# Sums of operands merged, the resolvent done by pairs, and the up product's second sum moved from ScalarE and GpSimd to VectorE

## What is computed

```python
def _s4_kernel(Lambda, p, q, B, Ct, step, L):
    g = 2.0 / step * ((1.0 - Omega) / (1.0 + Omega))
    denom = g[:, None] - Lambda[None, :]
    cauchy = lambda v: (v[None, :] / denom).sum(-1)
...
    at_roots = c * (k00 - k01 * (1.0 / (1.0 + k11)) * k10)
    return jnp.fft.ifft(at_roots, L).real
...
    g = jnp.einsum('bsh,ih->bsi', x, Wg)
    u = jnp.einsum('bsh,ih->bsi', x, Wu)
    h = jax.nn.silu(g) * u
    return jnp.einsum('bsi,hi->bsh', h, Wd)
```

## Time and profile before

| | |
|---|---|
| median of 3 runs | 1396.7 us (1395.41 to 1397.81) |
| the profiled execution | 1395.57 us, of which the span is 1393.4 us |
| TensorE busy | 1313.1 us, 94% |
| VectorE busy | 975.8 us, 70%; 98% from 200 to 500 us |
| ScalarE busy | 463.0 us, 33% |
| GpSimd busy | 687.9 us, 49%, all of it before 926 us |
| mean granted TensorE clock | 0.982 |

### The profile page before, as it was taken

One profiled execution on the slowest core, in us unless ns is written; L12 is line 12 of the kernel. 1 busy time (PEld: TensorE's weight loads), 2 busy tenths in 40 slices (PEclk: granted clock), 3 DMA queues, 4 the chain that ended last, 5 costly groups with the idle time before them and its releaser, 6 DMA issues.

```text
span 1393.4 us, 17064 instructions
## 1 busy us (share of the span) xinstructions
PE 1313.1 (94%) x6302; PEld 623.3 (45%) x6302; DVE 975.8 (70%) x1036; ACT 463.0 (33%) x827; POOL 687.9 (49%) x483
## 2 busy tenths in 40 slices
PE   3688899999999999899999999899999999999998
PEld 2444344444444444344444444344444444444444
DVE  7966799999999998879999898524343433241432
ACT  5744544455444455344454543410000000000000
POOL 6772777878787777668788896620000000000000
PEclk8799999999999999999999999999999999999999
DMA  8111545454555445444645543999554345336331
GB/s 311 34 46 38 165 142 155 133 179 140 168 146 162 138 136 175 117 155 130 179 137 176 157 144 114 334 414 310 165 189 149 98 151 183 104 109 219 99 98 61
DMA packets 165168, 218.09 MB, mean 157 GB/s; under 512 B 42204, under 2 KB 122718, under 8 KB 163166
## 3 DMA queue, kind: packets, MB, share of 16 engines
q1 hardware_dynamic: 163646, 200.69, 46.4%
q10 hardware_dynamic: 1440, 16.32, 2.9%
HBM read 139.64 MB, written 77.34 MB: 156 GB/s over the span
## 4 chain that ended last, share of the span: by engine, by line
PE 57%; DVE 3%; issue 1%; ACT 1%; DMA 0%; POOL 0%; SPq 0%; ACTq 0%; DVEq 0%
PE px L1461 16%; PE px L1375 13%; PE pz L1461 8%; PE pz L1375 6%; PE pv L1488 6%; PE py L1461 4%; PE py L1375 3%; DVE wf L1575 1%; DMA w_d<-ds 0%; DVE wf L1546 0%; DVE wf L1543 0%; DVE wf L1617 0%; DVE hf L1673 0%; DVE hf L1676 0%; POOL ds L696 0%
## 5 line engine op out<-in xcount | busy, mean ns | idle before, releaser
L1375 PE MATMUL px<-xo,wo 128*128 128x512 f16 x2016 | 464.2, 384 | 28.0 <-ACT u L997 21.3
L1375 PEld LDWEIGHTS px<-xo,wo 128*128 128x128 f16 x2016 | 197.4, 99 | 273.9 <-issue 26.0
L687 POOL TENSOR_TENSOR wo<-wf,wo 128x512 f16<-128x512 f32 x147 | 235.9, 1614 | 70.4 <-ACT wo L943 70.4
L706 POOL TENSOR_TENSOR hs<-hf,hs 128x512 f16<-128x512 f32 x154 | 215.4, 1405 | 108.5 <-ACT hs L978 108.3
L1461 PE MATMUL px<-wd,hr 128*128 128x512 f16 x1056 | 232.3, 379 | 0.0
L1375 PE MATMUL pz<-xo,wo 128*128 128x512 f16 x1008 | 231.3, 379 | 0.1
L1461 PEld LDWEIGHTS px<-wd,hr 128*128 128x128 f16 x1056 | 102.3, 98 | 118.7
L1375 PEld LDWEIGHTS pz<-xo,wo 128*128 128x128 f16 x1008 | 98.6, 98 | 118.4 <-issue 0.4
L943 ACT ACTIVATE wo<-wf 128x512 f16<-128x512 f32 x147 | 91.6, 624 | 102.5 <-DVE wf L1547 92.5
L978 ACT ACTIVATE hs<-hf 128x512 f16<-128x512 f32 x154 | 94.5, 621 | 89.6 <-DVE hf L1639 47.6
L1461 PE MATMUL pz<-wd,hr 128*128 128x512 f16 x528 | 116.6, 379 | 0.0
(11 more groups left out here) (229 smaller groups left out, 1417.4 us busy)
## 6 DMA issues: line engine op xcount, KB each, us to landing
h_d<-hs SPq DMA_DIRECT2D x154, 256.0 KB, 2.6
hr<-h_d SPq DMA_DIRECT2D x56, 704.0 KB, 4.4
w_d<-ds SPq DMA_DIRECT2D x73, 256.0 KB, 2.1
wd<-w_d ACTq DMA_DIRECT2D x4, 2816.0 KB, 15.5
sz<-in_sz_gate SPq DMA_DIRECT2D x21, 512.0 KB, 5.1
sz<-in_sz_up SPq DMA_DIRECT2D x21, 512.0 KB, 4.8
sz<-in_sz_down SPq DMA_DIRECT2D x20, 512.0 KB, 5.1
xc_d<-xo SPq DMA_DIRECT2D x8, 1024.0 KB, 7.6
```

The source lines that it names most:

```text
L687: pool.tensor_tensor(w_dest(t, j, 1), w_place_of(j), w_dest(t, j, 0), ALU.subtract).then_inc(wlo_done, 1)
L706: pool.tensor_tensor(hs[:, j, :, 1, :], h_place_of(p, j), hs[:, j, :, 0, :], ALU.subtract)\
L1375: done = pe.matmul(bank[:, :], wo[t % 2][:, j, wp, k * P:(k + 1) * P], xo[p][:, j, xp, k, :], start=(j in (0, 3) and k == 0 and wp == 0 an ...
```

## The change

1. **c22 to VectorE.** snap_u3 on ScalarE and the sum on GpSimd are gone. VectorE adds px (after turn 5) and s5 into u3 itself. TensorE's turn 7, which writes over px, now waits for this instruction. It stands behind s4_work(n) and ahead of c12(n).
2. **Fewer sums.** T1 and T3 of the weights are made by one instruction of twice the width, for gate and up and for down; so are S1 and S2 of h (h_s12, which now also waits for what only its second half waited for). S3 is taken with the other sign.
3. **Resolvent by pairs.** Two pieces at once, at n = 6, 11, 16 and 21, in seven instructions of 128x256. What follows comes a unit later: roots at 25, columns at 27, rows at 29, scale at 32. The angles are loaded in pairs.
4. **Tail.** The mask of the last words (`tail_words`) is a tensor_tensor with a tile of fifteens in place of a tensor_scalar.

```diff
             def c22(n):
-                pool.wait_ge(snap_done, 4 * full(n) + 4)
-                pool.tensor_tensor(u3[:, :], u3[:, :], s5[:, :], ALU.add).then_inc(u2_done, 1)
...
-            def snap_u3(n):
-                act.wait_ge(prod_done, products_before(n) + TURN_POS[4] + 1)
-                if n >= 1:
-                    act.wait_ge(hf_done, 2 * full_before(n) + 2)
-                act.activation(u3[:, :], px[n % 2][:, :], ACT.Copy).then_inc(snap_done, 1)
...
-                if j in (1, 2, 4, 5, 6):
-                    pe.wait_ge(snap_done, 4 * full(n) + {1: 1, 2: 1, 4: 3, 5: 2, 6: 4}[j])
+                if j in (1, 2, 4, 5):
+                    pe.wait_ge(snap_done, 3 * full(n) + {1: 1, 2: 1, 4: 3, 5: 2}[j])
+                if j == 6:
+                    pe.wait_ge(u2_done, full(n) + 1)
...
-                    link(dve.tensor_scalar(q[TAIL:P], r[TAIL:P], 15, None, ALU.bitwise_and))
+                    link(dve.tensor_tensor(q[TAIL:P], r[TAIL:P], fifteen[TAIL:P, :].broadcast_to((P - TAIL, 512)), ALU.bitwise_and))
...
                 if j == T1:
+
                     dve.wait_ge(deq_done, slab_up(t) + 1)
                     dve.wait_ge(wlo_done, base + W_POS[B11] + 1)
-                    dve.tensor_tensor(b11, b12, b11, ALU.subtract).then_inc(wsum_done, 1)
-                if j == T3:
-                    dve.tensor_tensor(b12, b22, b12, ALU.subtract).then_inc(wsum_done, 1)
+                    blocks = wf[:, :, :, :, :].rearrange("p s m n w -> p (s m n w)")[:, 0:10 * 256]\
+                        .rearrange("p (a b w) -> p a b w", a=2, b=5)
+                    dve.tensor_tensor(wf[:, 0, :, :, 0:256], wf[:, 0, 1:2, :, 0:256].broadcast_to((P, 2, 2, 256)),
+                                      blocks[:, :, 0:3:2, :], ALU.subtract).then_inc(wsum_done, 1)
...
+            def c22(n):
+                dve.wait_ge(prod_done, products_before(n) + TURN_POS[4] + 1)
+                dve.wait_ge(snap_done, 3 * full(n) + 2)
+                dve.tensor_tensor(u3[:, :], px[n % 2][:, :], s5[:, :], ALU.add).then_inc(u2_done, 1)
+
             def c12(n):
                 dve.wait_ge(prod_done, products_before(n) + TURN_POS[5] + 1)
-                dve.wait_ge(snap_done, 4 * full(n) + 3)
+                dve.wait_ge(snap_done, 3 * full(n) + 3)
...
                 dve.wait_ge(hf_done, 2 * n + 2)
                 if g == NG:
                     dve.wait_ge(hzero_done, p + 1)
-                dve.tensor_tensor(a21, a21, a22, ALU.add).then_inc(hsum_done, 1)
                 dve.wait_ge(hs3_done, q + 1)
                 dve.wait_ge(elo_done, 2 * q + 2)
-                dve.tensor_tensor(a, a22, a, ALU.subtract).then_inc(hsum_done, 1)
+
+                dve.tensor_tensor(hf[p][:, 0, :, :], hf[p][:, 0, :, :], hf[p][:, 1, 1:2, :].broadcast_to((P, 2, SB)),
+                                  ALU.add).then_inc(hsum_done, 1)
...
-                re, im, res = s4w[:, 0, :], s4w[:, 1, :], s4w[:, 2 + m % 2, :]
-                co, si = angle[m % 2][:, 0, :], angle[m % 2][:, 1, :]
...
+                dve.wait_ge(scaled_done, i + 1)
+                re, im, res = (s4w[:, k, :, :] for k in range(3))
+                co, si = angle[:, :, 0, :], angle[:, :, 1, :]
...
-                if n % 2 == 0 and 6 <= n < 6 + 2 * M8:
-                    resolvent((n - 6) // 2)
-                if n == 24:
+                if n in RESOLVENT:
+                    resolvent(RESOLVENT.index(n))
+                if n == 25:
                     cauchy_sums()
                     roots()
...
                 t_sum(2 * g + 1, T1)
-                t_sum(2 * g + 1, T3)
                 s4_work(n)
+                c22(n)
                 c12(n)
                 h_first(n, 2 * g, 0)
```

More of the change, by code:

```diff
@@ L46 @@
 LAST_POS = {j: i for i, j in enumerate(LAST_ORDER)}
-T_ORDER = (T1, T3, T2, T4)
-T_POS = {j: i for i, j in enumerate(T_ORDER)}
+T_ORDER = (T1, T2, T4)
+T_POS = {T1: 0, T3: 0, T2: 1, T4: 2}
 E_ORDER = (A11, S3)
@@ L253, in s4_plus_int4_swiglu @@
         below = small("below", [P, 1])
+        fifteen = small("fifteen", [P, 1], i32)
         par = small("par", [P, 5, 2])
@@ L267, in s4_plus_int4_swiglu @@
         ksc = small("ksc", [P, 3], i32)
-        angle = [at(f"angle{i}", [P, 2, P], f32, H0 + i * K1) for i in range(2)]
+        angle = at("angle", [P, 2, 2, P], f32, H0)
         flip = small("flip", [P, P])
         kshift = at("kshift", [P, 2, SB], f32, place[0])
-        s4w = small("s4w", [P, 4, P])
+        s4w = small("s4w", [P, 3, 2, P])
         dft = small("dft", [P, 2, P])
         twiddle = small("twiddle", [P, P])
+        zrow = at("zrow", [1, P], f32, place[0])
         krow = small("krow", [M8, 2, P // 2])
@@ L429, in store_xc, with load_angles @@
                              xo[p][:, j, :, :, :].rearrange("p a k s -> p (a k s)")).then_inc(xc_out, 16)
-            def load_angle(m):
-                if m == 0:
+            def load_angles(i):
+                if i == 0:
                     sp.wait_ge(xt_done, 56)
-                if m >= 2:
-                    sp.wait_ge(resolvent_done, m - 1)
-                sp.dma_start(angle[m % 2][:, :, :], angle_d[m:m + 1].broadcast_to((P, 2, P))).then_inc(angle_in[m % 2], 16)
+                else:
+                    sp.wait_ge(resolvent_done, i)
+                for h in range(2):
+                    m = 2 * i + h
+                    sp.dma_start(angle[:, h, :, :], angle_d[m:m + 1].broadcast_to((P, 2, P))).then_inc(angle_in[h], 16)
             load_x(0)
@@ L766, in _ @@
             w_low(1, T3)
-            c22(0)
             w_low(1, T2)
@@ L773, in _ @@
             x_sum_of(7, S4)
-            c22(1)
             h_low(0, 0, A11)
@@ L780, in _ @@
             d_low(0, B11)
-            c22(2)
             for j in (B11, B21):
@@ L791, in _ @@
                 w_low(2, j)
-            c22(3)
             d_low(0, B22)
@@ L807, in _ @@
                 d_low(g - 1, T4)
-                c22(n)
                 w_low(2 * g + 1, B22)
@@ L819, in _ @@
                 d_low(g - 1, T2)
-                c22(n + 1)
                 h_low(g - 1, 1, S4)
@@ L828, in _ @@
                 d_low(g, B21)
-                c22(n + 2)
                 w_low(2 * g + 2, B22)
@@ L838, in _ @@
                 w_low(2 * g + 2, T4)
-                c22(n + 3)
                 d_low(g, B22)
@@ L854, in _ @@
             d_low(NG - 1, T4)
-            c22(40)
             h_low(NG - 1, 1, S1)
@@ L879, in _ @@
             h_low(NG, 1, A22)
-            c22(43)
             for j in (A11, S3, S1, S2, S4):
@@ L1395, in s4_steps @@
             def s4_steps(n):
-                if n % 2 == 0 and 8 <= n < 8 + 2 * M8:
-                    m = (n - 8) // 2
-                    pe.wait_ge(resolvent_done, m + 1)
-                    pe.matmul(pv[0][:, 8 * m:8 * m + 8], s4w[:, 2 + m % 2, :], vw[:, :], start=True, stop=True)\
-                        .then_inc(cauchy_done, 1)
-                if n == 25:
+                if n - 2 in RESOLVENT:
+                    i = RESOLVENT.index(n - 2)
+                    pe.wait_ge(resolvent_done, i + 1)
+                    for h in range(2):
+                        pe.matmul(pv[0][:, 16 * i + 8 * h:16 * i + 8 * h + 8], s4w[:, 2, h, :], vw[:, :], start=True, stop=True)\
+                            .then_inc(cauchy_done, 1)
+                if n == 26:
                     pe.wait_ge(roots_done, 1)
@@ L1722, in numerators, with resolvent @@
                 dve.tensor_scalar(sc[NS:P, 6:7], sc[NS:P, 2:3], -1.0, None, ALU.mult).then_inc(numer_done, 1)
-            def resolvent(m):
+            def resolvent(i):
                 dve.wait_ge(numer_done, 1)
-                dve.wait_ge(scaled_done, m + 1)
-                re, im, res = s4w[:, 0, :], s4w[:, 1, :], s4w[:, 2 + m % 2, :]
-                co, si = angle[m % 2][:, 0, :], angle[m % 2][:, 1, :]
+                dve.wait_ge(scaled_done, i + 1)
+                re, im, res = (s4w[:, k, :, :] for k in range(3))
+                co, si = angle[:, :, 0, :], angle[:, :, 1, :]
                 dve.scalar_tensor_tensor(out=im, in0=co, scalar=sc[:, 4:5], in1=im, op0=ALU.mult, op1=ALU.add)
@@ L1862, in _ @@
             x_low(34)
-            t_sum(1, T3)
+            c22(0)
             c12(0)
@@ L1873, in _ @@
                 x_low(b)
+            c22(1)
             c12(1)
@@ L1884, in _ @@
             h_s12(0, 0)
+            c22(2)
             c12(2)
@@ L1892, in _ @@
             t_sum(2, T1)
-            t_sum(2, T3)
             t_sum(2, T2)
+            c22(3)
             c12(3)
@@ L1922, in _ @@
                 s4_work(n + 1)
+                c22(n + 1)
                 c12(n + 1)
@@ L1941, in _ @@
                 d_sum(g, T1)
[L1942 removed]
                 h_s4(g, 0)
                 s4_work(n + 3)
+                c22(n + 3)
                 c12(n + 3)
@@ L1957, in _ @@
             h_s4(NG - 1, 1)
+            c22(40)
             c12(40)
@@ L1970, in _ @@
             h_s4(NG, 0)
+            c22(43)
```

91 lines of the change are left out of this document (41 added, 50 removed).

## The result

The changed kernel takes 1465.9 us (median of 4 runs, 1464.5 to 1467.2), against 1396.1 of the kernel before on the same chip: 1.050 times as long, interval 1.0486 to 1.0511. The profiled execution took 1464.5 us, with a span of 1462.7 against 1393.4. The mean granted clock fell from 0.982 to 0.963.

A forecast was written before the change was run, and what follows sets the result against it. TensorE sets the end, with VectorE holding it back. To the profiled 1395.6 us the prediction added 70.3 for units 4 to 39 (102.1 of new waits and slow clock against today's 31.8) and 3 for units 40 to 43: 1469 us, range 1434 to 1492.

The forecast's parts named there:

- kind A: Six ordinary units (8, 12, 20, 24, 28, 36): turn 7 waits 3.1 us each for c22, 18.6 in all.
- M: Time from start of h_second to start of c22 in a unit; turn 7 waits M - 14.03 us.
- Kinds B and C: Units such as 21 (B) and 6 (C): B has 0.7 us to spare, C waits 0.2, before any S4 work.
- D: Units such as 11: VectorE is free early, so c22 has 1.1 us to spare before any S4 work.
- The S4 lumps: Resolvent pairs at 8.5 us each and later S4 steps, ahead of c22 in units 5 to 32: waits of 55.9 us.
- The clock: TensorE runs slower after waits: 1.8 us for each of seven long ones, 12.6, plus 5.4 for the six of 3.1.
- Unit 40: c22 10.6 us late at the tail's words; the new mask form saves 3, leaving about 7.4, with slow clock 9.2.
- The second half at nothing: After units 40 to 43 the forecast had no term: the second half was to cost nothing.
- Relief wins: Rival: c22 is never late and the waits for snap_u2 and the roots go; 1369 us, 5%.
- Only the S4 units wait: Rival: ordinary loop units don't wait because their stretch to c22 loses 3 us more than forecast; 1437 us, 13%.
- Everything waits more: Rival: pairs at 9.9 us, slow clock after every kind A wait, B and C 0.6 us later each; 1490 us, 14%.
- Cancel: Rival: gain and loss cancel, or turn 7 is not held in practice; 1397 us, 3%.

The follow-up runs named there:

- c22_back: Changed kernel with c22 put back as ScalarE's copy and GpSimd's sum, the other parts kept: 1405.6 us, 1.005 times the kernel before.
- loads_later: Changed kernel with ScalarE's acc and wd loads at the second half's start held until an hr load has landed: 1451.9 us, 1.040 times the kernel before.
- order_only: Kernel before, no work moved, plus a one-column memset ahead of c12 on VectorE on which TensorE's turn 7 waits: 1461.5 us, 1.047.
- c22_only: Kernel before with only c22 moved to VectorE; sums, resolvent pieces and mask as before: 1492.8 us, 1.069.
- pause_kept: c22_only with GpSimd waiting, where its c22 stood, until turn 5 is done, computing nothing there: 1482.6 us, 1.062 times the kernel before.

## Why the prediction was right, and where its parts were not

The 1465.9 us lie 3 below the 1469 forecast, and the profiled execution, for which the sum was made, 4.4 below it. The mechanism is the forecast one; but that the sum came out so near is luck: units 4 to 39 cost 18 us less than forecast, and the second half, which stood at nothing, cost 14.

- **The lateness of kind A: right.** M of 17.15 us was forecast, 17.24 measured. The six ordinary units of kind A waited 2.83 to 3.20 us by TensorE's rows, 18.7 together (forecast 18.6).
- **What shortened kind A: right sum, wrong terms.** M fell by 18.45 - 17.24 = 1.2 us (forecast 1.3). The forecast gave 1.0 of it to GpSimd's missing c22 and 0.3 to the merged sums. By the starts of VectorE's instructions, against the rows of unit 36, it is the other way round. From the sums of h to L1546 (L1532 now) 4.53 us became 3.51: the merged h_s12 gives 1.0. From there to T1 3.46 became 3.35: c22's absence gives 0.1, because the next low part of GpSimd fell beside that instruction instead (2.06 us where 2.17 had been). Merged T1 and T3 give 0.07. The two errors cancelled by luck.
- **Kinds B and C: too pessimistic.** C was to have M of 14.2 and has 12.3, the last 0.5 us of it a wait for turn 5; B was to have 13.3 and has the same 12.3, the last 1.5 a wait. So VectorE needs 11.9 and 10.8 us there. In B four instructions that had taken 0.8 to 1.0 us longer beside GpSimd now run undisturbed. D: 815.26 - 802.18 = 13.08, or 0.95 to spare (forecast 1.1).
- **The S4 lumps: mis-sized, and this is the largest miss.** Forecast 55.9 us; measured 3.6 (unit 5), 4.7 (6), 4.1 (11), 9.5 (16), 4.4 (21), 5.5 (25), 0.6 (27), 0 (29) and 4.4 (32), 36.8 in all. Two things made it. I took 8.5 us for a pair because GpSimd had been busy through a single piece; the pairs took 6.93 (unit 6), 5.18 (11), 6.92 (16) and 7.83 (21), 7 us less in all. At unit 16 three of its instructions took 1.3 us beside GpSimd, and then GpSimd's queue was dry and the sums took 0.41. The larger part, about 11 us, is the stretch ahead of the lumps in kinds B and C, as above. Unit 21, from h_second over the pair to c22:

```profile
519.18 0.69 DVE L1642 SCALAR_TENSOR_TENSOR hf<-u,sil 128x512 f32<-128x512 f32 x1 [3.17 <-ACT sil L1024]
...
529.90 0.47 DVE L1726 SCALAR_TENSOR_TENSOR s4w<-angle,sc,s4w 128x256 f32<-128x256 f32 x1
...
537.73 0.68 DVE L1616 TENSOR_TENSOR u<-px,s 128x512 f32<-128x512 f32 x1
```

Here 10.7 us stand ahead of the pair where the forecast had 13.3, and the same 10.7 in units 5 and 25. In c22_back, where more of GpSimd's work fell beside it, the pair at unit 21 took 8.9 us, as costed. So the price of a piece is that of its company, and one sample of a single piece didn't give it; nor did a stretch of the old order give the new one's length.

- **The clock: right.** Seven long waits were to cost 1.8 us each, 12.6. Their rows of 24 matmuls took 12.2 us more than 5.34 each. Of the six of kind A three lost 1.3 to 1.7 us and three nothing, 4.7 together (forecast 5.4).
- **Units 4 to 39: +52.0 us where +70.3 stood.** The difference of 18.3 is the S4 term (19) and smaller ones: C 1.6, unit 4 about 2 (24.18 us long, 6.05 too many, where 8 had been forecast), the clock 1. Against them stand the 0.2 us that each of 14 pauses is longer than its row says, 2.4, and 2.8 us that no term had: eight gaps of 0.1 to 0.5 us, most of them a small S4 matmul.
- **Unit 40: right in size by luck.** It waits 8.7 us (forecast 7.4; 10.6 - 3 is 7.6). The new form of the mask was to save 3 us. The form saved nothing; the mask took 6.17 instead of 7.14 for want of c22 beside it, and the two instructions behind it 0.69 each instead of 1.53, as GpSimd's queue was dry. Units 40 to 43 came out at +2.4 (forecast +3), unit 43's own wait gone as said.
- **The second half at nothing: wrong.** It lost 14.1 us, 12.25 of them in one pause. I looked for who waits for c22 in each unit and not for who waits for h_second of the last one: ScalarE's 7.7 MB of loads did. loads_later takes the 14 us away with one wait, and order_only, which leaves GpSimd's late c22 of unit 43 in place, never had them (c22_only has).
- **ScalarE and GpSimd relieved for nothing: right.** c22_back and order_only together show that neither the relief nor the cost of c22 decides.
- **The rivals.** "Relief wins" (1369) could not come in this order of work; with c22 and the S4 pieces in other places, 1383.9 is real, half of what it promised. "Only the S4 units wait" is out: kind A waits in every turn of the loop. "Everything waits more" is out: the pairs were shorter, the slow clock followed three of the six, and B and C were earlier, not later. "Cancel" is out.

What stays open: why the waits in units 10, 14 and 18 of pause_kept keep 2.2 us, which a stop tied to ScalarE's copy might settle; and which of ScalarE's loads (acc or wd) held the hr load up, since they were only moved together. In which of the parts 2 to 4 the 27 us of c22_only against the changed kernel lie wasn't tried one by one.
